# A post-norm decoder layer on one core: moving norm work, a table load and search steps between the engines

## The reference

```
x = layernorm(x + self_attention(x))      # 16 heads of 128, weights = codes * scales
x = layernorm(x + cross_attention(x, ctx))
    # scores = coef * (x @ Wq.T) @ ctx.T ; keep the 54 largest of 1024 in each row ;
    # softmax over those ; @ ctx ; @ Wo.T
x = layernorm(x + (silu(x @ Wg.T) * (x @ Wu.T)) @ Wd.T)   # inner width 2048
layernorm(x) = (x - mean) / sqrt(var + 1e-5)
```

## Time and profile before

| what | value |
| --- | --- |
| median of 3 runs | 939.14 us (938.7 to 939.49) |
| the profiled execution's own time | 938.63 us |
| its span | 936.8 us |
| PE busy | 910.6 us, 97% |
| VectorE busy | 588.8 us, 63% |
| ScalarE busy | 579.8 us, 62% |
| GpSimd busy | 503.0 us, 54% |
| mean TensorE clock granted | 0.995 of full speed |
| stage 1 / stage 2 up to the first RIGHT product | about 0 to 534 us / about 508 to 607 us |

### The profile page before, as it was taken

One profiled execution on the slowest core, in us unless ns is written; L12 is line 12 of the kernel. 1 busy time (PEld: TensorE's weight loads), 2 busy tenths in 40 slices (PEclk: granted clock), 3 DMA queues, 4 the chain that ended last, 5 costly groups with the idle time before them and its releaser, 6 DMA issues.

```text
span 936.8 us, 13231 instructions
## 1 busy us (share of the span) xinstructions
PE 910.6 (97%) x4440; PEld 749.9 (80%) x4440; DVE 588.8 (63%) x1059; ACT 579.8 (62%) x1150; POOL 503.0 (54%) x413
## 2 busy tenths in 40 slices
PE   9999999999999999999989999799999999999997
PEld 7788788887788877887768788698888788888885
DVE  5666966678666776667584899976697125411114
ACT  4667876688766878787875566443745535433333
POOL 4357652646626467377754568534574852354440
PEclk9999999999999999999999999899999999999999
DMA  7532230122301322113112213332333341343221
GB/s 203 157 96 63 75 101 1 51 69 74 103 1 32 88 68 76 61 57 91 46 57 90 80 35 102 88 94 75 117 112 102 114 123 34 114 125 96 93 80 45
DMA packets 46102, 76.97 MB, mean 82 GB/s; under 512 B 5584, under 2 KB 11216, under 8 KB 45776
## 3 DMA queue, kind: packets, MB, share of 16 engines
q1 hardware_dynamic: 45600, 75.68, 27.2%
q10 hardware_dynamic: 432, 0.39, 0.2%
HBM read 73.69 MB, written 2.36 MB: 81 GB/s over the span
## 4 chain that ended last, share of the span: by engine, by line
PE 30%; DVE 15%; ACT 3%; issue 3%; POOL 1%; ACTq 0%; DVEq 0%; POOLq 0%
DVE m L1586 5%; PE p L899 4%; PE p L903 4%; PE p L900 4%; DVE SX L1594 2%; DVE SCL L1594 2%; PE p L913 2%; PE p L915 2%; PE p L914 2%; PE p L865 1%; DVE SX L1597 1%; PE p L866 1%; PE p L867 1%; DVE SX L1836 1%; DVE st L1546 1%
## 5 line engine op out<-in xcount | busy, mean ns | idle before, releaser
L2013 POOL TENSOR_TENSOR V<-RAW,V 128x512 fp32r<-128x512 f32 x64 | 85.5, 1359 | 131.0 <-ACT V L1082 131.0
L1513 DVE TENSOR_SCALAR_CACHE_REDUCE JK<-p,ssc 128x512 bf16<-128x512 f32 x112 | 83.7, 747 | 112.8 <-PE p L664 112.8
L1025 ACT ACTIVATE PR<-p,nms,ssc 128x512 f32<-128x512 f32 x112 | 87.4, 780 | 59.3 <-DVE JK L1513 58.0
L2009 POOL TENSOR_TENSOR acc<-SX,acc 128x512 f32<-128x512 f32 x56 | 72.4, 1293 | 82.3 <-ACT SX L1062 51.3
L682 PE MATMUL p<-R 128*128 128x512 f32 x248 | 97.3, 392 | 0.8 <-DVE V L1506 0.8
L2013 POOL TENSOR_TENSOR C<-RAW,C 128x512 fp32r<-128x512 f32 x58 | 75.3, 1310 | 31.2 <-ACT C L1082 31.2
L1836 DVE TENSOR_TENSOR SX<-p,SX 128x512 f32<-128x512 f32 x32 | 22.0, 689 | 110.2 <-PE p L903 95.5
L1526 DVE TENSOR_TENSOR PT<-p,PT 128x512 fp32r<-128x512 f32 x128 | 87.3, 682 | 5.4 <-ACT PT L1044 5.2
L717 PEld LDWEIGHTS p<-ident,PR 128*128 128x128 f32 x512 | 62.4, 140 | 21.2 <-DVE PT L1526 6.6
L717 PE MATMUL p<-ident,PR 128*128 128x128 f32 x512 | 77.4, 274 | 1.0
L1044 ACT ACTIVATE PT<-p 128x512 fp32r<-128x512 f32 x128 | 75.8, 592 | 0.0
(11 more groups left out here) (249 smaller groups left out, 2750.2 us busy)
## 6 DMA issues: line engine op xcount, KB each, us to landing
RAW<-in_wg SPq DMA_DIRECT2D x32, 256.0 KB, 2.8
RAW<-in_wu SPq DMA_DIRECT2D x32, 256.0 KB, 2.6
RAW<-in_ctxn SPq DMA_DIRECT2D x32, 256.0 KB, 2.8
RAW<-in_wd SPq DMA_DIRECT2D x32, 256.0 KB, 2.7
RAW<-in_wq SPq DMA_DIRECT2D x19, 256.0 KB, 2.7
RAW<-in_wk SPq DMA_DIRECT2D x18, 256.0 KB, 2.7
RAW<-in_wv SPq DMA_DIRECT2D x16, 256.0 KB, 2.7
RAW<-in_wo SPq DMA_DIRECT2D x16, 256.0 KB, 5.1
```

What stands on the lines that cost most here:

```text
L1025: e.activation(PR[:, i % 2, :], P[i % 2][:, :], ACT.Exp, bias=nms[:, i % 4:i % 4 + 1], scale=ssc[:, 0:1] if HB[j][0] > 1 else SC, accum_ou ...
L1513: e.tensor_scalar(JK[:, :], P[i % 2][:, :], ssc[:, 1:2] if HB[i // 4][0] > 1 else -SC, None, ALU.mult, ALU.min, accum_out=nms[:, i % 4:i % ...
L2009: e.tensor_tensor(acc[:, r], scaled_at(4 * q + tt), acc[:, r], ALU.add).then_inc(*rows[r].up((q, 1)))
L2013: e.tensor_tensor(lo, RAW[:, slot[key], :], hi, ALU.subtract).then_inc(*c_lo.up(key))
```

## The change

`scaled_by_act` now also sends the h = 1 additions of q = 13, row blocks 2 and 3, to ScalarE and GpSimd. In quarter 119 ScalarE loads the square root's table before it waits for the statistics. VectorE norms batch 0's row blocks 0, 1 in quarter 119 and 2, 3 in quarter 120 (before: 120 and 121). After the loop VectorE no longer norms row blocks 4 and 5; it makes their `ln_bias`, and ScalarE applies it before `xs_copy(3, 0, 0)`; the semaphore `norm_bias` now counts by pair of row blocks. The search takes three steps instead of two in quarter 126 and one more after `ot_low(31)`; `o_add(15, 2, 0)` is done ahead of the statistics of rows 4 and 5; later calls of `run` are shifted by the same counts. On ScalarE the numbers in `run` follow, and `qx_high(1, 3)` now stands behind two further search steps.

```diff
--- before.py
+++ after.py
@@ -270,7 +270,7 @@
 
 def scaled_by_act(q, tt, h):
 
-    return h == 1 and (q not in (13, 15) or (q == 13) == (tt < 2))
+    return h == 1 and (q < 15 or tt >= 2)
 
 
 def decoder_layer(nc, xT, xn, wq, sq, wk, sk, wv, sv, wo, so, bqk, bv, bo,
@@ -1148,7 +1148,7 @@
                 return s
 
             def ln1_apply(r):
-                w.wait_ge(*norm_bias.at())
+                w.wait_ge(*norm_bias.at(r - r % 2))
                 e.activation(acc[:, r], acc[:, r], ACT.Identity, bias=nms[:, r - 4:r - 3],
                              scale=rstd[:, r:r + 1]).then_inc(*rows[r].up("ln1"))
 
@@ -1249,6 +1249,7 @@
                 if j in (28, 29) and qt >= 2:
                     conv_xw(0, 2 * (j - 28) + qt - 2)
                 if (j, qt) == (29, 3):
+                    act_table(ACT.Sqrt)
                     ln_std(1, 0, 4)
                 if j == 30 and qt in (1, 2):
                     for r in (2 * qt - 2, 2 * qt - 1):
@@ -1262,7 +1263,7 @@
                 if i in (125, 126):
                     for hf in range(2):
                         xs_copy(i - 125, hf, BANK["xs", i - 125, hf])
-                    search(topk.run(i - 124))
+                    search(topk.run((1, 3)[i - 125]))
                 if i >= 126:
                     for n in (2 * (i - 126), 2 * (i - 126) + 1):
                         conv_ct(1, n)
@@ -1280,6 +1281,8 @@
             for tt in (2, 3):
                 o_scale(NJ // 2 - 1, tt)
             ln_std(1, 4, 2)
+            ln1_apply(4)
+            ln1_apply(5)
             xs_copy(3, 0, 0)
             search(topk.run(2))
             x2_high(4, False)
@@ -1287,7 +1290,7 @@
             x2_high(5, False)
             ln1_apply(6)
             ln1_apply(7)
-            search(topk.run(2))
+            search(topk.run(3))
             xs_copy(3, 1, 1)
             conv_ct(1, 7)
             search(topk.run(2))
@@ -1296,11 +1299,10 @@
             act_table(ACT.Exp)
             conv_gu(0)
             search(topk.run(2))
-            for m in range(3):
+            for m in range(4):
                 search(topk.run(2))
                 qx_high(1, m)
-            qx_high(1, 3)
-            search(topk.run(6))
+            search(topk.run(4))
             conv_gu(1)
             for n, hf, k in ((4, 0, 2), (4, 1, 3)):
                 xs_copy(n, hf, k)
@@ -1558,7 +1560,7 @@
                 w.wait_ge(*rstds.at((1, r)))
                 w.wait_ge(*sexp.at(127))
                 e.scalar_tensor_tensor(out=nms[:, r - 4:r - 2], in0=mv[:, r:r + 2, 0], scalar=-1.0,
-                                       in1=rstd[:, r:r + 2], op0=ALU.mult, op1=ALU.mult).then_inc(*norm_bias.up())
+                                       in1=rstd[:, r:r + 2], op0=ALU.mult, op1=ALU.mult).then_inc(*norm_bias.up(r))
 
             def ln_apply(key, r, r0):
                 w.wait_ge(*rstds.at((key, r0)))
@@ -1748,8 +1750,8 @@
                 if (j, qt) == (29, 3):
                     ln_stats(1, [2, 3], row_writers(2)[-6])
                     ln_rstd(1, 0, 4)
-                if j == 30 and qt < 2:
-                    for r in (2 * qt, 2 * qt + 1):
+                if i in (119, 120):
+                    for r in (2 * (i - 119), 2 * (i - 119) + 1):
                         ln_apply(1, r, 0)
                 if j == 30 and qt in (1, 2):
                     for r in (2 * qt - 2, 2 * qt - 1):
@@ -1768,20 +1770,18 @@
             topk.ready.add(2)
             search(topk.run(1))
             ot_low(NJ - 1)
+            search(topk.run(1))
             for tt in range(2):
                 for h in range(2):
                     o_add(NJ // 2 - 1, tt, h)
+            o_add(NJ // 2 - 1, 2, 0)
             ln_stats(1, [4, 5], (15, 1))
-            o_add(NJ // 2 - 1, 2, 0)
             o_add(NJ // 2 - 1, 3, 0)
-            ln_rstd(1, 4, 2)
-            ln_apply(1, 4, 4)
-            ln_apply(1, 5, 4)
+            ln_bias(4)
             search(topk.run(1))
             ln_stats(1, [6, 7], (15, 1))
-            search(topk.run(1))
             ln_bias(6)
-            search(topk.run(3))
+            search(topk.run(4))
             topk.ready.add(3)
             search(topk.run(2))
             search(topk.run(4))
```

## The result

| what | before | after |
| --- | --- | --- |
| median of 7 runs, alternating | 939.49 us (938.7 to 940.88) | 944.79 us (944.39 to 948.86) |
| ratio, 95% interval | | 1.0065 [1.0054, 1.0076] |
| the profiled execution's own time, its span | 938.63, 936.8 us | 945.96, 944.2 us |

The changed kernel is slower, by 0.65% by the ratio and by 5.3 us between the medians. I had forecast 937.6 us, within 934.6 to 940.4.

A forecast was written before the change was run, and what follows sets the result against it. TensorE, busy for 97% of the span, was taken as the bound, so only its idle time could be won. Batch 0's norm (0.6) plus the way to the RIGHT product (0.9) gave 1.5 us: median 937.6 us, range 934.6 to 940.4.

The forecast's parts named there:

- Part 1: Batch 0's norm, quarters 118 to 123: table load ahead of the root and earlier applies bring `q_proj` 0.6 us sooner.
- the gain that I counted at `x2_low`: Batch 0's norm: `x2_low` no longer behind the second pair of applies, starting near 486.8, 0.65 us sooner.
- Part 2: Quarter 126 and behind `ot_low`: two search steps fit VectorE's idle time and delay nobody, 2.3 us ahead.
- Part 3: Batch 1's norm, rows 4 and 5 on ScalarE: `q_proj` won 1.7 us, VectorE back at the search 2.2 sooner.
- Part 4: Search step (0,13) in front of `qx_high(1,3)`: TensorE gives back 0.6 us at `x_scores(4,0)`, 1.1 stays won.
- Part 5: To the first RIGHT product: `x_out` 2.6 us sooner, but tile 3's exponential behind `px_high(2)` leaves 0.9 won.
- C: Slower: tile 3's exponential behind `px_high(2)`, TensorE not ahead at `x_out`; 940.3, up to 942.2 us; chance 0.15.

The follow-up runs named there:

- e2: Changed kernel, but GpSimd waits in quarter 119, behind row 4's bias, until VectorE has normed row block 1; 944.81 us, ratio 1.0052.
- e9: Kernel before, with only batch 1's row blocks 4 and 5 normed on ScalarE and `o_add(15,2,0)` ahead of their statistics; 937.83 us, ratio 0.9982.
- e1: Changed kernel, with tile 3's exponential ahead of `px_high(2)` on ScalarE; 943.25 us, ratio 1.0035.
- e8: Changed kernel without its quarters 118 to 120 part, tile 3's exponential ahead of `px_high(2)`, last query copy ahead of tile 0's exponential; 939.46 us, ratio 0.9996.
- e15: Kernel before, with the table loaded ahead and the applies in quarters 119 and 120, products left on VectorE; 940.68 us, ratio 1.0015.
- e14: Kernel before, with row blocks 4 and 5 on ScalarE, the table loaded ahead and one search step behind `ot_low(31)`; 935.29 us, ratio 0.9958.
- e7: Changed kernel without its part in quarters 118 to 120, and with tile 3's exponential ahead of `px_high(2)`; 941.03 us, ratio 1.0011.
- e3: Changed kernel without its part in quarters 118 to 120 (products, table, earlier applies); 942.95 us, ratio 1.0034.
- e4: Kernel before, with only the change's part in quarters 118 to 120 (products, table, earlier applies); 943.44 us, ratio 1.0045.

## Why the prediction was wrong

**Part 1, order.** Right: the addition that waits (473.91), the bias behind it (475.17), `o_add(13,3,0)` behind that (I said 475.75, it was 476.57, of which 0.57 is the head), the load ahead of the root, `proj_o(14,0)` waiting for `qk_low`. The root came at 480.83; with the head taken out that is 0.16 later than my 480.1, and the reciprocal 0.43 later.

**Part 1, cost. Failed:** "the applies of rows 0, 1 then end at 481.2 (0.95 for both)". I took the duration from the earlier trace rows, where GpSimd was idle, and moved the instruction to where GpSimd has two additions. It is 3.05 us there (e2: 1.00 with GpSimd held off). That is 2.06 of the 3.2 us by which this stretch missed. With the 0.43 of the reciprocal it makes `proj_o(14,0)` late by 2.5. The last 0.7 is the gain that I counted at `x2_low`: TensorE's matmuls from 489.2 to 492 ran at 1.2 GHz (granted 0.50) behind its waits of 1.41 and 2.09 us, a term that I had put at nothing. The hint was among my own rows: the same pair is 0.99 in the earlier trace rows and 2.37 in the earlier trace rows. I used both figures and did not ask why they differ.

**Part 2.** Right: in front of the two `o_add` VectorE now idles 0.46 and 0.49 us instead of 1.79 and 1.63, and the stretch to batch 1's `q_proj` gained what was forecast. **Part 3.** Right: -1.67 against -1.7; e9 shows it as the gain it is.

**Part 4.** The order was right (the copy behind the exponential, TensorE's wait of 0.62 at L780 against my 0.6). **Failed:** twelve steps and (0,12) "end at 554.85", and behind them "(1,14) ends at 564.6". On that clock, with the 3.14 us by which batch 0's `q_proj` was late taken out, they ended at 555.4 and 567.3. The small product was held (0.97), then the masks of tiles 0 and 1 (2.23 and 2.37, where my count has one plain step each, 1.28 at most): 2.9 us in all, against the 2.7 by which `x_out` came later than forecast (+1.82 against -0.9).

**Part 5.** "VectorE idles 2.2 us" was right (2.13), as was the exponential behind `px_high(2)`. **Failed:** "masks to 602.65", 1.3 us; it took 2.31 beside a low part of GpSimd's. With the clock's 1.56 us at `x_out`, which this execution had, this is the 2.6 between +4.36 and +1.75.

**The rivals.** C came true in its mechanism and its side: the exponential of tile 3 behind `px_high(2)` with TensorE not ahead at `x_out` (it started 2.7 us later than before, after the mark's 0.57). Its price was too low, 940.3 to 942.2 against 944.8, since C too had unheld masks, and its cause was another. The sum in part 5 from which it came shows terms that add up to 605.3, not 605.5; the 0.25 us between a mask's end and the transposes, which the forecast has, is not written in it. Taking the order back (e1) leaves 3.3 us of loss; taking back the order, the copy and part 1 (e8) leaves none, with the gain of the norm's move (e9, 1.7 us) in it, so the moved steps still cost some 1.3 us there.

The Trainium skill, "SBUF — State Buffer", section "Who interferes with whom", says that VectorE and GpSimd share a port pair under an exclusive lock, held for a whole instruction. By it a VectorE instruction with two SBUF inputs contends with a GpSimd one that reads SBUF, and so does one in a mode that uses both ports, while one with at most one input from SBUF outside these modes doesn't. The trace agrees on both sides: masks and applies are held (1.28 to 2.37, 0.99 for a pair to 3.05), and the search (1.20 to 1.23 throughout) and the statistics (1.28 for a pair) are not. Which mode the applies ran in no row shows. I did not weigh this rule in the forecast, and it was the one that spoke against the change.

**The range** reached to 940.4 and gave slower than before 0.12. Every bound in it moved waits about and none lengthened an instruction; the cover that I named for the moved work was an engine's idle time, and not the state of the neighbour it shares SBUF with.

## What to carry to other kernels

When one instruction form has two durations in a trace, find out what runs beside it before using either; an instruction of such a form is to be priced by what GpSimd does at its new place, not at its old one. A quarter sooner the same pair of applies took 2.38 (e15) or 3.05 us instead of 0.99. Moving such applies to ScalarE, where each took 0.80 to 0.82 us beside GpSimd's work (after, from 540.17), took 2.37 us off VectorE and not the 0.99 of an unheld pair. Before adding steps in front of a list, check that the other engine walking the same sequence doesn't meet its step behind something that now takes longer.

## What the runs showed of the hardware

- The hold between VectorE and GpSimd works in both directions: a mask of 1.28 us took up to 2.37, and GpSimd's pair of low parts beside it 3.5 instead of 2.5 us (e1, after).
- Size doesn't protect: the product of 128 x 2 elements took 0.16 us alone and 0.31, 0.61 and 0.97 beside GpSimd's low parts (e9, e14, after), depending on how much of one was left: in after the product ends at 544.62 and GpSimd's part, begun at 543.32 and some 1.25 us long, at 544.57.
- A table load took 1.28 us and the next activation started 1.29 us after the load's start.
- TensorE's clock fell to a granted 0.50 (1.2 GHz) behind waits of some 0.4 and 1.73 us in the profiles of after, e2, e7 and e8, and not in e1 and e3 with the same waits. In quarters 121 and 122 it fell behind waits of 1.4 and 2.1 us in all three profiles that have both (after, e1, e4), and not in e15 (0.23 and 2.09) and e2 (2.85 alone). One profile doesn't give the price of the clock. The profiled executions differ by 7.3 us and the medians by 5.3; how many of the timed runs had such a fall isn't known.
